# The last attention and feed-forward of a four-layer model: row work folded together, and the first rows started in the stage before

## The reference

```python
def _L3_xattn_ref(q, k, v, mask, ...):          # q is the layer norm of x, k and v the context
    Q, K, V = (_split_heads(_linear(...)) ...)    # 16 heads of 16
    score = jnp.einsum('bhqd,bhkd->bhqk', Q, K) / dk
    attn = jnp.where(mask, -jnp.inf, score)       # no softmax
    o = _linear(ctx, wo_w, wo_b)
    x = residual + o                              # residual is q
    return ln_g * (x - mu) * jax.lax.rsqrt(var + LN_EPS) + ln_b

def _L3_ffn_ref(x, w1, b1, w2, b2):              # x is the layer norm of the residual
    def rmsnorm(x): return x * jax.lax.rsqrt(jnp.mean(x * x, axis=-1, keepdims=True) + EPS)
    def act_quant(x):                             # to 8 bits, one scale for each row
        scale = 127.0 / jnp.clip(jnp.max(jnp.abs(x), axis=-1, keepdims=True), 1e-05)
        return jnp.clip(jnp.round(x * scale), -128.0, 127.0) / scale
    def bitlinear(x, w, b):
        return jnp.einsum('bsd,fd->bsf', act_quant(rmsnorm(x)), weight_quant(w)) + b
    return bitlinear(gelu(bitlinear(x, w1, b1)), w2, b2)   # 256 -> 1024 -> 256
```

## Time and profile before

| what | us |
|---|---|
| median of 3 runs | 2030.05 (2016.5 to 2032.82) |
| the profiled execution | 2016.93 |
| its span | 2015.0 |
| PE busy | 1650.0 (82%) |
| DVE busy | 1079.7 (54%) |
| ACT busy | 905.6 (45%) |
| POOL busy | 364.3 (18%) |

### The profile page before, as it was taken

The page is one execution under the profiler, slowest core; times in us unless marked ns, Lnnn a source line. Parts: engine busy times, 40 slices in busy tenths (PEclk is TensorE's granted clock), DMA queues, the critical chain, the costliest instruction groups (busy, mean ns, idle before and its releaser), DMA issues.

```text
span 2015.0 us, 27743 instructions
## 1 busy us (share of the span) xinstructions
PE 1650.0 (82%) x9994; PEld 1241.9 (62%) x10002; DVE 1079.7 (54%) x3154; ACT 905.6 (45%) x2021; POOL 364.3 (18%) x465
## 2 busy tenths in 40 slices
PE   6888854999669999999868899999996799858165
PEld 4666654878646666666537667776666578847033
DVE  6766641222265665566576465555555244237796
ACT  4787711222136565555554155555550022212298
POOL 1000012001132323223110100000001512223633
PEclk9999966999879999999979999999996899988566
DMA  9000026767500000000000200000000468860000
GB/s 312 1 1 2 1 92 226 274 241 268 192 16 11 7 6 6 6 1 1 1 1 0 74 11 6 6 6 6 1 1 18 168 206 276 302 229 0 0 11 32
DMA packets 52695, 152.24 MB, mean 76 GB/s; under 512 B 7968, under 2 KB 38704, under 8 KB 44272
## 3 DMA queue, kind: packets, MB, share of 16 engines
q1 hardware_dynamic: 45168, 133.90, 19.6%
q0 software_dynamic: 5280, 14.47, 1.9%
q10 hardware_dynamic: 2112, 2.10, 0.3%
HBM read 133.89 MB, written 24.75 MB: 79 GB/s over the span
## 4 chain that ended last, share of the span: by engine, by line
PE 56%; DVE 13%; ACT 12%; DMA 8%; issue 5%; POOL 4%; POOLq 1%; another core or an unknown queue 0%; SPq 0%; DVEq 0%; ACTq 0%
PE bank L1335 6%; PE bank L1348 6%; PE bank L1281 5%; PE bank L904 5%; PE bank L860 5%; PE bank L1322 4%; PE bank L1285 4%; PE bank L1265 3%; PE bank L1687 3%; ACT l L684 3%; DMA WB<-in_L2pack 3%; DMA WB<-in_L0pack 3%; ACT p1f L1401 2%; POOL small L206 2%; PE bank L1677 1%
## 5 line engine op out<-in xcount | busy, mean ns | idle before, releaser
L1530 DVE TENSOR_REDUCE small<-bank 128x1 f32<-128x512 f32 x128 | 82.4, 686 | 108.7 <-PE bank L1335 108.7
L1526 DVE CUSTOM_DVE_ANT_0 p1f<-bank,p1f 128x512 f32<-128x512 f32 x128 | 83.2, 687 | 103.4 <-PE bank L1335 103.4
L1401 ACT ACTIVATE p1f<-p1f,small 128x512 f32<-128x512 f32 x128 | 91.4, 714 | 101.1 <-DVE small L1526 101.1
L923 ACT ACTIVATE e2a<-bank,WB 128x128 f32<-128x128 f32 x156 | 44.6, 369 | 204.0 <-PE bank L904 185.7
L684 ACT ACTIVATE l<-l,small 128x256 f32<-128x256 f32 x256 | 110.2, 499 | 46.1 <-DVE small L749 46.0
L1404 ACT ACTIVATE p2f<-bank,small 128x512 f32<-128x512 f32 x128 | 86.9, 683 | 86.2 <-DVE small L1530 86.2
L348 POOL TENSOR_SCALAR rs<-mv 128x4 f32<-128x4 f32 x20 | 4.8, 240 | 604.4 <-DVEq L226 563.2
L1281 PE MATMUL bank<-WA,HT 128*128 128x256 f32 x384 | 94.3, 389 | 9.6 <-DVE p1f L1471 9.6
L749 DVE CUSTOM_DVE_ANT_0 l<-bank,small 128x256 f32<-128x256 f32 x256 | 90.6, 419 | 16.4 <-PE bank L629 16.0
L923 ACT ACTIVATE e0a<-bank,WB 128x128 f32<-128x128 f32 x128 | 36.6, 368 | 134.0 <-PE bank L904 134.0
L1415 ACT ACTIVATE p2f<-bank 128x512 f32<-128x512 f32 x128 | 75.2, 598 | 40.5 <-PE bank L1322 39.0
(11 more groups left out here) (379 smaller groups left out, 4038.2 us busy)
## 6 DMA issues: line engine op xcount, KB each, us to landing
WB<-in_L2pack SPq DMA_DIRECT2D x39, 1026.0 KB
WB<-in_L0pack SPq DMA_DIRECT2D x16, 2052.0 KB
e0a<-in_L0pack SPq DMA_DIRECT2D x7, 2052.0 KB
sorted_h<-in_blank SPq DMA_DIRECT2D x6, 1032.0 KB, 16.7
e2a<-sorted_h SPq DMA_DIRECT2D x39, 129.0 KB
e2a<-given_y SPq DMA_DIRECT2D x8, 512.0 KB, 7.4
e0a<-sorted_h SPq DMA_DIRECT2D x23, 129.0 KB
WB<-in_ctx ACTq DMA_DIRECT2D x4, 512.0 KB, 8.8
```

Source lines behind the costliest of these rows:

```text
L1401: ins = a.e.activation(P, P, ACT.Exp, scale=-1.0, bias=self.mx[:, m:m + 1], accum_out=self.sm[:, m:m + 1])
```

## The change

In the last attention the penalty is added to `Hn` by ScalarE (`penalty`, four tiles after each group's transposes) and the bias `bo` by GpSimd (`added`, four tiles in one instruction), so that VectorE adds the bank and `Hn` in one instruction for a block; its residual and GpSimd's `lng` and `lnb` also take a block in one instruction. In the feed-forward the first chain's norm and root mean square become one factor from the variance (`factor`), and its limits are made for four tiles at once (`limits`). The second chain's inverse and limit are folded into one factor with which VectorE rounds. Both chains transpose the rounded float32 values, and `MAGIC` comes off as ScalarE copies them out of the bank. Rows 0 to 3 of the feed-forward and their limits are made in block 7 of the attention's loop, with their factor on GpSimd in block 5 and the first rounding at the end of ScalarE's part. Banks: 6 for the first transposes, 4 and 5 for the second, 7 alone for the second matmul (it was 6 and 7).

```diff
-    def ac(self, a):
+    def ac(self, a, behind=None):
         k = self.k
         for g in range(4):
+            if behind and g:
+                behind(g - 1)
...
+    def po(self, g, behind=None):
         k, eps = self.k, 1e-5
         for j in range(4):
+            if behind and j >= 2:
+                behind(j - 2)
...
+        if behind:
+            behind(2)
+            behind(3)
...
+        self.norm.ac(a, lambda j: self.penalty(a, j))
...
+        self.next.early_ac(a)
...
+            if i == 7:
+                self.next.early_dv(v)
             b = i
             if b < 8:
-                bk, y = k.bank(self.R.bank(("O", b))), self.rows_of(b)
+                bk, y = k.bank(self.R.bank(("O", b))), self.ys[b % 3]
                 v.wait_ge(self.om, b + 1)
-                v.wait_ge(self.penned, 1)
+                v.wait_ge(self.hb, b // 2 + 1)
                 v.wait_ge(self.res, b - 2)
...
+                v.e.tensor_tensor(y, bk.rearrange("p (a n) -> p a n", a=2), self.Hn[:, 2 * b:2 * b + 2, :], ALU.add).then_inc(self.od.sem, 1)
...
                 v.wait_ge(self.st, b + 1)
...
             b = i - 2
             if 0 <= b < 8:
...
+                x = k.X[:, 2 * b:2 * b + 2, :]
                 v.wait_ge(self.ya, b + 1)
-                k.residual(v, 2 * b, y[0], self.heir)
-                k.residual(v, 2 * b + 1, y[1], self.heir, (self.res, b + 1))
-
-    def rows_of(self, b):
-        return [self.ys[2 * b % 6 + a] for a in range(2)]
+                v.e.tensor_tensor(x, self.ys[b % 3], x, ALU.add).then_inc(self.res.sem, 1)
+                v.wait_ge(self.res, b + 1)
+                for a in range(2):
+                    ins = v.e.bn_stats(k.st[:, (2 * b + a) % 8, :], x[:, a, :])
+                v.chain(ins)
+                for a in range(2):
+                    ins = v.e.bn_aggr(k.mv[:, 2 * b + a, :], k.st[:, (2 * b + a) % 8, :])
+                if b % 2:
+                    ins.then_inc(k.stat_of[self.heir].sem, 1)
...
+    def added(self, g, j):
+
+        k = self.k
+        h = self.Hn[:, 4 * j:4 * j + 4, :]
+        g.wait_ge(self.ha, j + 1)
+        g.e.tensor_tensor(h, h, k.row("bo").rearrange("p (o n) -> p o n", o=1).to_broadcast([128, 4, 256]), ALU.add).then_inc(self.hb.sem, 1)
+
+    def penalty(self, a, j):
+        a.wait_ge(self.norm.tr, 2 * j + 2)
+        a.wait_ge(self.penned, 1)
+        for t in range(4 * j, 4 * j + 4):
+            ins = a.e.activation(self.Hn[:, t, :], self.Hn[:, t, :], ACT.Identity, bias=self.pen[:, t:t + 1])
+        ins.then_inc(self.ha.sem, 1)
...
-        self.norm.po(g)
+        self.norm.po(g, lambda j: self.added(g, j))
         for i in range(9):
             if i < 8:
                 g.wait_ge(self.st, i + 1)
                 k.rstd(g, k.rs[:, 2 * i:2 * i + 2], k.mv2[:, 2 * i:2 * i + 2, 1], 2, self.rn)
+            if i == 5:
+                self.next.factor(g, 0)
             b = i - 1
             if b < 0:
                 continue
             g.wait_ge(self.yn, b + 1)
...
+            y = self.ys[b % 3]
+            w, s = (k.row(n).rearrange("p (o n) -> p o n", o=1).to_broadcast([128, 2, 256]) for n in ("lng", "lnb"))
+            g.chain(g.e.tensor_tensor(y, y, w, ALU.mult))
+            g.e.tensor_tensor(y, y, s, ALU.add).then_inc(self.ya.sem, 1)
...
-    SEGS = 25
+
+    AT = (("x", -15), ("cut", -14), ("rnd", -3), ("tx", -2), ("ex", -1), ("up", 3), ("deq", 4), ("gelu", 5), ("sq", 6), ("top", 6),
+          ("pow", 7), ("fac", 8), ("rndh", 9), ("th", 10), ("eh", 11), ("down", 12), ("y", 13), ("add", 14))
...
+        for step in range(-1, 3 * 15 + 15):
             for t in range(16):
-                if 0 <= step - 3 * t < self.SEGS:
-                    yield t, step - 3 * t
+                for what, at in self.AT:
+                    if step == max(3 * t + at, -1) and (what != "cut" or t % 4 == 3):
+                        yield t, what
...
+    def early_dv(self, v):
+
+        for i in range(4):
+            self.row(v, i)
+        self.limits(v, 3)
+
+    def early_ac(self, a):
+        self.round(a, 0)
+
+    def factor(self, g, i):
+
+        k, eps = self.k, 1e-5
+        rs, var = k.rs2[:, 4 * i:4 * i + 4], k.mv[:, 4 * i:4 * i + 4, 1]
+        g.wait_ge(self.stat, i + 1)
+        g.chain(g.e.tensor_scalar(rs, var, 1.0 + eps, eps * eps, ALU.mult, ALU.add))
+        g.e.tensor_tensor(rs, rs, k.nhalf[:, 0:4], ALU.pow).then_inc(self.rn.sem, 1)
+
+    def row(self, v, i):
+        k, x = self.k, self.xs[i % 8]
+        v.wait_ge(self.rn, i // 4 + 1)
+        v.wait_ge(self.xtr, i - 7)
+        v.e.tensor_scalar(x, k.X[:, i, :], k.mv[:, i, 0:1], k.rs2[:, i:i + 1], ALU.subtract, ALU.mult).then_inc(self.xn.sem, 1)
+        v.wait_ge(self.xn, i + 1)
+        v.e.tensor_reduce(self.xtop[:, i:i + 1], x, AX.X, ALU.max, apply_absolute_value=True).then_inc(self.xtops.sem, 1)
+
+    def limits(self, v, i):
+        e = v.e
+        top, inv, out = (c[:, i - 3:i + 1] for c in (self.xtop, self.xinv, self.xout))
+        v.wait_ge(self.wsc, 1)
+        v.wait_ge(self.xtops, i + 1)
+        v.chain(e.tensor_scalar(top, top, 1e-5, None, ALU.max))
+        v.chain(e.reciprocal(inv, top))
+        e.tensor_scalar(out, top, self.sc[:, 2:3], 1.0 / 127.0, ALU.mult, ALU.mult)
+        e.tensor_scalar(inv, inv, 127.0, None, ALU.mult).then_inc(self.xcut.sem, 1)
+
+    def round(self, a, i):
+        a.wait_ge(self.xcut, i // 4 + 1)
+        a.e.activation(self.xs[i % 8], self.xs[i % 8], ACT.Copy, scale=self.xinv[:, i:i + 1], bias=MAGIC).then_inc(self.xrnd.sem, 1)
...
+            if s == "tx":
+                t.wait_ge(self.xrnd, i + 1)
+                t.wait_ge(self.xev, i)
+                for c in range(2):
+                    ins = t.e.transpose(k.bank(6)[:, c * 128:(c + 1) * 128], self.xs[i % 8][:, c * 128:(c + 1) * 128], k.ident[:, :])
+                ins.then_inc(self.xtr.sem, 1)
+            elif s == "up":
...
+            elif s == "th":
+                t.wait_ge(self.hrnd, i + 1)
+                t.wait_ge(self.hev, i)
+                for c in range(8):
+                    ins = t.e.transpose(k.bank(4 + c // 4)[:, c % 4 * 128:(c % 4 + 1) * 128], self.hs[i % 4][:, c * 128:(c + 1) * 128], k.ident[:, :])
+                ins.then_inc(self.htr.sem, 1)
...
-                t.wait_ge(self.yd, i - 1)
+                t.wait_ge(self.yd, i)
...
+            if s == "rnd" and i > 0:
+                self.round(a, i)
+            elif s == "ex":
+                a.wait_ge(self.xtr, i + 1)
+                a.wait_ge(self.up, i - 2)
+                a.e.activation(self.xT[i % 3], k.bank(6)[:, 0:256].rearrange("p (k n) -> p k n", k=2), ACT.Copy, bias=-MAGIC).then_inc(self.xev.sem, 1)
...
+            elif s == "sq":
+                a.wait_ge(self.gel, i + 1)
+                a.wait_ge(self.sqr, i - 1)
+                a.e.activation(self.scr[i % 2], self.hs[i % 4], ACT.Square, accum_out=self.hss[:, i:i + 1]).then_inc(self.sqr.sem, 1)
+            elif s == "eh":
+                a.wait_ge(self.htr, i + 1)
+                a.wait_ge(self.dn, i - 2)
+                for x in range(2):
+                    ins = a.e.activation(self.hT[i % 3][:, 4 * x:4 * x + 4, :], k.bank(4 + x).rearrange("p (k n) -> p k n", k=4), ACT.Copy, bias=-MAGIC)
+                ins.then_inc(self.hev.sem, 1)
...
+            elif s == "deq":
+                h = self.hs[i % 4]
                 v.wait_ge(self.up, i + 1)
...
+                v.wait_ge(self.htr, i - 3)
+                v.wait_ge(self.sqr, i - 3)
+                v.wait_ge(self.xcut, i // 4 + 1)
...
+            elif s == "top":
+                v.wait_ge(self.gel, i + 1)
+                e.tensor_reduce(self.htop[:, i:i + 1], self.hs[i % 4], AX.X, ALU.max, apply_absolute_value=True).then_inc(self.top.sem, 1)
+            elif s == "fac":
+                v.wait_ge(self.pow, i + 1)
+                v.chain(e.reciprocal(self.hinv[:, i:i + 1], self.hcut[:, i:i + 1]))
+                e.tensor_scalar(self.hfac[:, i:i + 1], self.hinv[:, i:i + 1], self.hss[:, i:i + 1], 127.0, ALU.mult, ALU.mult).then_inc(self.fac.sem, 1)
+            elif s == "rndh":
+                v.wait_ge(self.fac, i + 1)
+                v.wait_ge(self.sqr, i + 1)
+                e.tensor_scalar(self.hs[i % 4], self.hs[i % 4], self.hfac[:, i:i + 1], MAGIC, ALU.mult, ALU.add).then_inc(self.hrnd.sem, 1)
...
+        for i in range(1, 4):
+            self.factor(g, i)
         for i, s in self.walk():
...
+            if s == "pow":
+                r, cut = self.hss[:, i:i + 1], self.hcut[:, i:i + 1]
+                g.wait_ge(self.sqr, i + 1)
+                g.chain(g.e.tensor_scalar(r, r, 1.0 / 1024, eps, ALU.mult, ALU.add))
+                g.chain(g.e.tensor_tensor(r, r, k.nhalf[:, 0:1], ALU.pow))
+                g.wait_ge(self.top, i + 1)
+                g.chain(g.e.tensor_scalar(cut, self.htop[:, i:i + 1], r, 1e-5, ALU.mult, ALU.max))
```

(40 more changed lines are left out.)

130 lines of the change are left out of this document (24 added, 106 removed).

## The result

| | before | after |
|---|---|---|
| median, us | 2023.67 (2016.5 to 2032.82) | 1986.31 (1982.09 to 1991.01) |
| the profiled execution, us | 2016.93 | 1984.45 |
| ratio | | 0.983, 95% interval 0.980 to 0.987 |

What follows compares the result with a forecast made beforehand. ScalarE was taken to bound the feed-forward, VectorE close behind, and VectorE the attention's loop. Attention -5.0, joint -8.2, loop -5.3 and drain -5.3 gave -24, from the median of 2030 to 2006 us; range 1986 to 2024.

Steps and rivals of the forecast that it cites:

- Attention: Last attention: shorter block periods, early feed-forward rows, a shorter end and a costlier start, together -5.0 us.
- The rival of wide additions: Attention: GpSimd's 1024-wide additions block VectorE, 6.0 us a block, start costing 5; 2018 us in all, chance 0.12.
- The start: Before the attention's loop: GpSimd's wide bias addition stands in line and disturbs VectorE, +2.5 us, bounds 0.5 and 5.
- Joint: Between attention and feed-forward: 12.4 us shrink to 4.2 because tiles 0 to 3 are already made, saving 8.2.
- the rival that they only move work: Joint and attention's loop: early rows move work one for one, shrinking the 8.2 us saved by 4.4; no separate chance.
- Loop: Feed-forward's 15 periods: VectorE 5.1 us a tile at full clock, 6.7 at half, 70% full; 82.5 against 87.84, -5.3.
- The rival of full clock throughout: Feed-forward: TensorE's ring never binds, loop 75 us, drain -6.1; 1998 us in all, chance 0.25.
- The half-clock ring: Feed-forward loop on TensorE: second matmul, first matmul, transposes and copies close one tile's ring, 6.7 us at half clock.
- the rival's 2022: Feed-forward at half clock throughout: loop 97 us, drain -4.4; 2022 us in all, chance 0.18.
- Drain: From the last dequantization to the span's end: 15.2 to 17 us against 21.35, saving 5.3, bounds 4.4 and 6.1.
- the slower rival: Feed-forward: GpSimd's four small steps, X in sum, wait behind VectorE, deciding from X = 3.4; 2047 us, chance 0.05.
- One sign: Feed-forward loop: `L2224` waiting for `L2287` at full clock was named as something that would show the forecast wrong.

Runs made afterwards that it cites:

- experiment 2: Changed kernel with feed-forward rows 0 to 3, their factor, limits and first rounding made behind the feed-forward's fence; ratio to the kernel before 0.981, four pieces' sum 175.58 us.
- experiment 3: New feed-forward with the old last attention, rows 0 to 3 behind the fence; ratio to the kernel before 0.984, feed-forward loop 70.93 us.
- 7: Changed kernel with every second of the second chain's eight float32 transposes left out; feed-forward loop 68.66 us, clock 0.89.
- Experiment 4: Changed kernel with ScalarE taking the rounding constant off into bfloat16 ahead of both transposes, which run in bfloat16; feed-forward loop 85.65 us, clock 0.74.
- 5: Kernel before with 8 and 2 extra float32 transposes behind each tile's own; feed-forward loop 88.02 us, clock 0.88.
- 6: Kernel before with as many extra float32 matmuls of a constant behind each chain's own transposes; feed-forward loop 88.05 us, clock 0.96.
- 8: Changed kernel with the norm of feed-forward rows 4 to 15 on ScalarE, behind square and rounding; ratio to the kernel before 0.984, loop 73.26 us.
- 9: Changed kernel with the norm of feed-forward rows 7 to 15 on ScalarE, ahead of each tile's GELU; ratio to the kernel before 0.981, loop 68.11 us.

## Why the prediction was right in direction and short in size

**Attention.** The sum came out (-6.2 for -5.0), the bound did not: the prediction named GpSimd with 4.45 a block, and it is TensorE with 4.32, for which 4.2 was put. GpSimd stays under that because `L2067` takes 1.26 where 1.36 was put (not within the 1.3 to 1.5 named). The two limits lie so close that the period was hardly touched. The rival of wide additions (6.0 a block, 5 at the start) falls. The start was put at +2.5 and cost 1 to 2; the early rows took 5.3 in place of 4.4, their first two norms being stretched to 1.27 and 0.97. Alone the attention gives 11 to 12.5, and hands 5 to 7 back for the early rows.

**Joint.** As worked out, 4.18 for 4.2. But 6 of its 8.2 are the early rows', so the rival that they only move work (5) is shown by experiment 2; it was in the sum.

**Loop.** This term was mis-sized, 82.5 for 69.38. After's periods are 4.44, 4.94, 5.02, 5.40, 4.83, 5.33, three of 4.83, 4.56, and five of 4.05 to 4.11. Nine of them have a row to make (4.83) and six have none (4.07), since rows are made over six tiles ahead of the dequantization; the second, sixth and tenth hold the limits of four tiles, 0.5 more. So VectorE's list is 9 x 4.83 + 6 x 4.07 + 3 x 0.5 = 69.4, where 15 x 5.1 = 76.5 was put. First, a period with a row was put 0.27 too long, above all by the stretched 0.66 for a norm of 0.41: 2.4 us. Second, the prediction gave every tile the whole list, and six periods have no row: 6 x (5.1 - 4.07) = 6.2 us, less 1.5 for the limits, which its 5.1 had spread over all: 4.7. Third, the share of full clock: 70% was put, which costs 15 x 0.3 x 1.6 = 7.2 less 1.5 for the first tiles, 5.7. But the measured loop is no longer than the bare list: the third and fourth period cost 0.8 over it at half clock, and the first two are 0.8 under it. These make 12.8 of the 13.1. The rival of full clock throughout was nearest, and had the first two errors too.

**The half-clock ring** was real where it could be seen. In the other profiled execution of after, one turn closes at half clock, from second matmul to second matmul:

```profile
1896.81 1.89 PE L2231 MATMUL bank<-WA,f3a 128*128 128x256 bf16 x8 [0.75 <-ACT f3a L2256]
1898.49 1.91 PE L2217 MATMUL bank<-WA,f3a 128*128 128x512 bf16 x4
1900.20 1.74 PE L2224 MATMUL bank<-ident,WB 128*128 128x128 f32 x8
...
1903.12 1.05 PE L2231 MATMUL bank<-WA,f3a 128*128 128x256 bf16 x8 [0.96 <-ACT f3a L2256]
```

It took 6.31 with the clock rising within it, for 6.7. In experiment 3 all of TensorE's work in the turn lies at half clock, and it took 6.48 (`L2206` is the second matmul there):

```profile
1927.64 1.89 PE L2206 MATMUL bank<-WA,f3a 128*128 128x256 bf16 x8 [0.75 <-ACT f3a L2232]
...
1934.12 1.05 PE L2206 MATMUL bank<-WA,f3a 128*128 128x256 bf16 x8 [0.75 <-ACT f3a L2232]
```

So the ring's size was right to 0.2 us. Then the clock was full. In four profiles (both of after, experiments 3 and 7) it rose in the first such turn, in which TensorE works without a gap; whether that brings the clock back is not shown, and no run held the ring apart from the clock. A loop at half clock throughout was never seen, and the rival's 2022 stays untested.

**Drain.** 16.36, within 15.2 to 17 (14.67 in experiment 2, with the same drain). **GpSimd's chain** (the slower rival): X is 1.3 and `L2282` waits for it only in the drain, so it is refuted at its own point. One sign was badly chosen: at full clock `L2224` does wait for `L2287`, by 0.25 to 0.88 us in five tiles one after another.

```profile
1938.94 1.09 PE L2224 MATMUL bank<-ident,WB 128*128 128x128 f32 x8 [0.25 <-DVE WB L2287]
```

A bound by VectorE means just that; it speaks against nothing.

**Slips in the sums**, none of which moves the forecast by more than 0.3 us: the drain's terms make 15.0 to 16.7, GpSimd's block 4.42, the chance of faster 0.55 and of the same 0.40 with the three quarters named; and the slower rival's +6 in the drain is counted against the forecast's drain, not the old one.

**Where the gain comes from.** Experiment 4 shows what can't be left out: without transposing the float32 values and taking `MAGIC` off in the copy, 16 of the loop's 18.5 us are lost. Whether that alone, with the old factor, would give them is untested. The clock's rise is not a gain by itself (5, 6). That it keeps the ring short enough for VectorE to be the bound is argued from the ring's 6.48 at half clock against VectorE's 4.83; no run shows it alone.

## What to carry to other kernels

List the new bound's work tile by tile and not as a mean: steps that run ahead are absent from the last tiles. A duration read from a trace may be a stretched one: look for the shortest of its kind, and at what ran beside it. A pass on the bounding engine that also stands in the chain ahead of TensorE can cost twice, by its length and by the clock (0.74 for 0.92 in experiment 4); how the two divide wasn't measured. A step moved to an idle engine must stand where that engine idles (experiments 8 and 9: the same instruction, periods of 5.45 and 4.38), and work moved out of a joint into the end of the stage before, where it stands in line too, gained nothing that could be seen.
